# High and low value columns of a head side by side in one stationary operand, the cross part added on VectorE

## The reference

```
x: [8, 256, 256], ctx: [8, 256, 256]
h = layernorm(x)
h = layernorm(h + attention(h, h,   mask))       # 16 heads of 64
h = layernorm(h + attention(h, ctx, mask))
h = layernorm(h + gelu(h @ fc1_w + fc1_b) @ fc2_w + fc2_b)
x = x + h
y = layernorm(x)
x = x + geglu(y, shared) + geglu(y, expert chosen by argmax(y @ Wg))   # 8 experts

attention(x, c, mask):
    q, k, v = x @ wq, c @ wk, c @ wv
    out = softmax(mask(q @ k.T / 8)) @ v         # per head
    return out @ wo + bo
```

## Time and profile before

| | us |
|---|---|
| median of 3 runs | 1401.46 |
| the profiled execution | 1397.69 |
| its span, first to last instruction | 1395.9 |
| PE busy | 1353.5 |
| DVE busy | 965.5 |
| ACT busy | 815.4 |
| POOL busy | 532.1 |
| mean granted TensorE clock | 0.991 of full |

### The profile page before, as it was taken

The page is one execution under the profiler, slowest core; times in us unless marked ns, Lnnn a source line. Parts: engine busy times, 40 slices in busy tenths (PEclk is TensorE's granted clock), DMA queues, the critical chain, the costliest instruction groups (busy, mean ns, idle before and its releaser), DMA issues.

```text
span 1395.9 us, 32853 instructions
## 1 busy us (share of the span) xinstructions
PE 1353.5 (97%) x11598; PEld 1305.0 (93%) x11598; DVE 965.5 (69%) x2677; ACT 815.4 (58%) x2212; POOL 532.1 (38%) x913
## 2 busy tenths in 40 slices
PE   4999999999999999999999989999999999999999
PEld 3899999999998999999999989899999999999998
DVE  5777777777787777777777784434447777777754
ACT  3666766666666666766676665333226656565632
POOL 3644535444467444443443577655150000000040
PEclk9999999999999999999999999999999999999999
DMA  5060000000000004000000101010044666566521
GB/s 173 2 247 16 12 7 17 17 1 17 24 2 24 24 2 174 24 2 24 24 9 17 32 4 43 31 31 8 2 166 140 201 212 210 191 204 212 197 69 62
DMA packets 65185, 100.30 MB, mean 72 GB/s; under 512 B 4736, under 2 KB 53504, under 8 KB 65024
## 3 DMA queue, kind: packets, MB, share of 16 engines
q1 hardware_dynamic: 63488, 94.00, 20.2%
q0 software_dynamic: 1536, 4.20, 0.9%
HBM read 81.93 MB, written 16.25 MB: 70 GB/s over the span
## 4 chain that ended last, share of the span: by engine, by line
PE 88%; POOL 5%; DVE 3%; ACT 2%; issue 2%; DVEq 0%; ACTq 0%; POOLq 0%
PE ps_pj L47 10%; PE ps_pj L48 9%; PE ps_pj L49 9%; PE ps_t L797 9%; PE ps_s L787 7%; PE ps_pv L47 6%; PE ps_pv L49 6%; PE ps_pv L48 6%; PE ps_s L47 4%; PE ps_aux L47 4%; PE ps_aux L48 4%; PE ps_aux L49 4%; PE ps_s L49 4%; PE ps_s L48 4%; PE ps_t L830 1%
## 5 line engine op out<-in xcount | busy, mean ns | idle before, releaser
L555 POOL TENSOR_SCALAR probs<-probs,inv 128x256 f32<-128x256 f32 x512 | 241.9, 487 | 387.8 <-DVE inv L1227 387.5
L1028 ACT ACTIVATE probs<-scores,nb 128x256 f32<-128x256 f32 x512 | 255.1, 500 | 227.8 <-DVE nb L1217 213.2
L1217 DVE CUSTOM_DVE_ANT_0 scores<-ps_s,maskf 128x256 f32<-128x256 f32 x512 | 187.0, 421 | 64.8 <-PE ps_s L787 63.6
L1231 DVE TENSOR_TENSOR probs_t_lo<-ps_t,probs_t_hi 128x512 fp32r<-128x512 f32 x256 | 175.6, 686 | 14.1 <-ACT probs_t_hi L1035 2.6
L1089 ACT ACTIVATE gelu<-ps_pj 128x512 f32<-128x512 f32 x92 | 55.0, 598 | 189.0 <-PE ps_pj L49 189.0
L797 PE MATMUL ps_t<-ident,probs 128*128 128x128 f32 x1024 | 142.6, 282 | 12.2 <-POOL probs L555 12.2
L1277 DVE TENSOR_TENSOR ps_s<-ps_s,gelu 128x512 f32<-128x512 f32 x92 | 64.4, 700 | 126.2 <-PE ps_s L49 126.1
L1035 ACT ACTIVATE probs_t_hi<-ps_t 128x512 fp32r<-128x512 f32 x256 | 148.5, 580 | 3.3 <-PE ps_t L797 3.3
L47 PE MATMUL ps_pv<-probs_t_hi,vpad_lo 128*128 128x256 f32 x512 | 145.5, 284 | 0.0
L48 PE MATMUL ps_pv<-probs_t_lo,vpad_hi 128*128 128x256 f32 x512 | 145.2, 283 | 0.0
L49 PE MATMUL ps_pv<-probs_t_hi,vpad_hi 128*128 128x256 f32 x512 | 145.1, 283 | 0.0
(11 more groups left out here) (228 smaller groups left out, 4706.9 us busy)
## 6 DMA issues: line engine op xcount, KB each, us to landing
raw<-in_L_ffn_W SPq DMA_DIRECT2D x45, 1024.0 KB, 4.8
slot_rows<-hin SPq DMA_DIRECT2D x5, 768.0 KB, 7.2
xin<-slot_rows SPq DMA_DIRECT2D x15, 256.0 KB, 6.2
slot_out<-hin SPq DMA_DIRECT2D x15, 256.0 KB, 6.0
rows<-in_x SPq DMA_DIRECT2D x8, 256.0 KB, 2.7
after_self<-rows SPq DMA_DIRECT2D x8, 256.0 KB, 2.1
rows<-after_self SPq DMA_DIRECT2D x8, 256.0 KB, 2.6
cin<-in_ctx SPq DMA_DIRECT2D x8, 256.0 KB, 3.0
```

What stands on the lines that cost most here:

```text
L555: last = pool.tensor_scalar(PR[:, h, t, :], PR[:, h, t, :], inv[:, h, t:t + 1], 1.0, ALU.mult, ALU.mult)
L1028: last = act.activation(PR[:, h, t, :], SM[:, h, t, :], ACT.Exp, bias=nb[:, h, t:t + 1], scale=-1.0, accum_out=sums[:, h, t:t + 1])
L1217: last = dve.tensor_tensor_reduce(SM[:, h, t, :], ps_s[h][:, t * S:(t + 1) * S], maskf[:, i // PAIRS % 2, :], -SCALE, -LOWEST, ALU.add, AL ...
L1231: dve.tensor_tensor(flat(PT[1][:, i % 2, h, :, :]), ps_t[h][:, :], flat(PT[0][:, i % 2, h, :, :]).bitcast(F32), ALU.subtract).then_inc(t_l ...
```

## The change

`VP`, the padded values, becomes `VS`: for each head and block of keys one stationary operand of 128 columns, of which the first 64 are the high parts of the values and the last 64 their low parts. `attend` multiplies it by the low and then by the high part of the probabilities, and gives each head 256 columns of `ps_pv`. Rows 0 to 63 then hold the high values by the whole probabilities, rows 64 to 127 the low values by them, which is the cross part (with low by low, which was left out before).

ACT copies rows 64 to 127 of the bank into `cross` (`cross_of_pair`). DVE adds them to rows 0 to 63 in `joined`, one addition for each head (`join_pair`). `hi_of_pair` and `lo_of_pair` now read `joined` in SBUF, one pair later, and stand at other places of the loops. The values are split with one instruction of 128x512 on each engine in place of two of 128x256, and the clears at the start are gone.

```diff
             def attend(i):
                 g, p = i // 2, i % PAIRS
                 pe.wait_ge(pj_lo, EVENT[("v", g)] + 1)
-                wait(pe, o_lo, i)
+                wait(pe, joined_ready, i)
                 for h in range(2):
                     pe.wait_ge(t_lo, 2 * i + h + 1)
                     for j in range(ST):
-                        last = product(pe, ps_pv[:, 0:S], tuple(v[:, g % 2, j, 2 * (i % 2) + h, :] for v in VP),
-                                       tuple(x[:, i % 2, h, j, :] for x in PT), h == 0 and j == 0, h == 1 and j == ST - 1)
+                        v = VS[:, g % 2, j, 2 * (i % 2) + h, :, :].rearrange("p s d -> p (s d)")
+                        for x in (PT[1], PT[0]):
+                            last = pe.matmul(ps_pv[:, h * S:(h + 1) * S], v, x[:, i % 2, h, j, :], start=h == 0 and j == 0 and x is PT[1],
+                                             stop=j == ST - 1 and x is PT[0], skip_group_check=True)
                 last.then_inc(pv_done, 1)
...
-                    for odd in range(2):
-                        last = act.activation(vpad_half(VP[0], k, odd), v_half(bank, odd), ACT.Copy)
+                    last = act.activation(v_part(k, 0), v_rows(bank), ACT.Copy)
...
+            def cross_of_pair(i):
+                act.wait_ge(pv_done, i + 1)
+                act.activation(flat(cross[:, :, :]), ps_pv[DH:P, :], ACT.Copy).then_inc(cross_ready, 1)
+
             def hi_of_pair(i):
-                act.wait_ge(pv_done, i + 1)
+                act.wait_ge(joined_ready, i + 1)
                 wait(act, out_done, i - 3)
-                act.activation(OT[0][:, i % 4, :], ps_pv[:, 0:S], ACT.Copy).then_inc(o_hi, 1)
+                act.activation(OT[0][:, i % 4, :], joined[:, i % 2, :], ACT.Copy).then_inc(o_hi, 1)
...
                 hi_of_probs(i, 0)
+                if i >= 2:
+                    hi_of_pair(i - 2)
                 if i + 1 < NPAIR:
                     exps(i + 1, 1)
                 if i + 2 < NPAIR:
                     hi_of_bank(("qk", i + 2))
                 hi_of_probs(i, 1)
                 if i >= 1:
-                    hi_of_pair(i - 1)
+                    cross_of_pair(i - 1)
...
+            hi_of_pair(NPAIR - 2)
             gelu_dense(0)
+            cross_of_pair(NPAIR - 1)
             hi_of_pair(NPAIR - 1)
...
-                    for odd in range(2):
-                        last = dve.tensor_tensor(vpad_half(VP[1], k, odd), v_half(bank, odd),
-                                                 vpad_half(VP[0], k, odd).bitcast(F32), ALU.subtract)
+                    last = dve.tensor_tensor(v_part(k, 1), v_rows(bank), v_part(k, 0).bitcast(F32), ALU.subtract)
...
+            def join_pair(i):
+
+                dve.wait_ge(cross_ready, i + 1)
+                for h in range(2):
+                    last = dve.tensor_tensor(joined[h * DH:(h + 1) * DH, i % 2, :], ps_pv[0:DH, h * S:(h + 1) * S], cross[:, h, :], ALU.add)
+                last.then_inc(joined_ready, 1)
+
             def lo_of_pair(i):
                 dve.wait_ge(o_hi, i + 1)
-                dve.tensor_tensor(OT[1][:, i % 4, :], ps_pv[:, 0:S], OT[0][:, i % 4, :].bitcast(F32),
+                dve.tensor_tensor(OT[1][:, i % 4, :], joined[:, i % 2, :], OT[0][:, i % 4, :].bitcast(F32),
                                   ALU.subtract).then_inc(o_lo, 1)
...
-            for vp in VP:
-                dve.memset(vp[:, :, :, :, :].rearrange("p a b c d -> p (a b c d)").bitcast(F32), 0.0).then_inc(pad_ready, 1)
...
                 lo_of_probs(i, 0)
+                if i >= 2:
+                    lo_of_pair(i - 2)
                 if i + 1 < NPAIR:
                     invert_sums(i + 1, 1)
                 if i + 2 < NPAIR:
                     lo_of_bank(("qk", i + 2))
                 lo_of_probs(i, 1)
                 if i >= 1:
-                    lo_of_pair(i - 1)
+                    join_pair(i - 1)
...
+            lo_of_pair(NPAIR - 2)
+            late_hi_pieces(NPAIR + 1)
+            join_pair(NPAIR - 1)
             lo_of_pair(NPAIR - 1)
-            late_hi_pieces(NPAIR + 1)
```

More of the change, by code:

```diff
@@ L220, in fused @@
         PT = at("probs_t_hi", 104 * KB, [P, 2, 2, ST, S], F32R), at("probs_t_lo", 112 * KB, [P, 2, 2, ST, S], F32R)
-        VP = at("vpad_hi", 120 * KB, [P, 2, ST, HG, P], F32R), at("vpad_lo", 128 * KB, [P, 2, ST, HG, P], F32R)
+        VS = at("v_stack", 120 * KB, [P, 2, ST, HG, 2, DH], F32R)
+        cross, joined = at("cross", 128 * KB, [DH, 2, S]), at("joined", 130 * KB, [P, 2, S])
         QK = at("qk_hi", 136 * KB, [P, 2, 2, S], F32R), at("qk_lo", 144 * KB, [P, 2, 2, S], F32R)
@@ L257, in fused @@
         WB = [(W["k"], W["v"], tuple(t[:, :, :, :, :].rearrange("p a b c d -> p (a b c d)") for t in PT)),
-              (W["q"], W["o"], tuple(t[:, :, :, :, :].rearrange("p a b c d -> p (a b c d)") for t in VP))]
+              (W["q"], W["o"], (at("w3b_hi", 120 * KB, [P, WCOLS], F32R), at("w3b_lo", 128 * KB, [P, WCOLS], F32R)))]
         x2, normed = (stage[:, k * TT * D:(k + 1) * TT * D].rearrange("p (t d) -> p t d", d=D) for k in range(2))
@@ L295, in fused @@
         const_in, mask_in = sem("const_in"), sem("mask_in")
-        id_ready, pad_ready, half_ready, mask_ready = sem("id_ready"), sem("pad_ready"), sem("half_ready"), sem("mask_ready")
+        id_ready, half_ready, mask_ready = sem("id_ready"), sem("half_ready"), sem("mask_ready")
         first_in = {(k, q): sem(f"first_{k}{q}") for k in KINDS for q in range(GROUPS)}
@@ L308, in fused @@
         t_done, t_hi, t_lo = sem("t_done"), sem("t_hi"), sem("t_lo")
-        pv_done, o_hi, o_lo = sem("pv_done"), sem("o_hi"), sem("o_lo")
+        pv_done, cross_ready, joined_ready, o_hi, o_lo = (sem(n) for n in ("pv_done", "cross_ready", "joined_ready", "o_hi", "o_lo"))
         out_done, out_used = sem("out_done"), sem("out_used")
@@ L987, in _, with v_part, v_rows @@
                     down(step, range(FC))
[L989 to L994, removed]
+        def v_part(g, s):
+            return VS[:, g % 2, :, :, s, :].rearrange("p t h d -> p (t h) d")
+        def v_rows(bank):
+            return bank[:, :].rearrange("p (a d) -> p a d", d=DH)
         def flat(ap):
@@ L1011, in hi_of_bank @@
                 if kind == "v":
-                    if k == 0:
-                        act.wait_ge(pad_ready, 2)
                     wait(act, pv_done, 2 * (k - 1))
-                    for odd in range(2):
-                        last = act.activation(vpad_half(VP[0], k, odd), v_half(bank, odd), ACT.Copy)
+                    last = act.activation(v_part(k, 0), v_rows(bank), ACT.Copy)
                 elif kind == "qk":
```

## The result

The changed kernel takes 1435.54 us, the median of 4 runs (1434.51 to 1435.97), against 1401.32 us before (1401.15 to 1401.79, 4 runs). The ratio is 1.0243, with a 95% interval of 1.0225 to 1.026: 34 us slower. The span of the profiled execution went from 1395.9 to 1434.2 us, 38.3 us more; the profiled execution of before lay 3.6 us under its median, which is most of the difference between 34 and 38.

A forecast was written before the change was run, and what follows sets the result against it. PE was taken to bound attention at 6.23 us a plain pair, by only 0.33 us. Added ring work of 90.3 less 69.8 slack, +5 from the second ring and -2.5 at the start gave +23: 1424 us, range 1400 to 1442.

The forecast's parts named there:

- PE's step of 0.12 us, and 61 us taken from it: Attention, PE: a removed matmul gives back its 0.12 us step, not its 0.28 length; four per pair, 61 us in all.
- The two rings, 5.42 and 5.90 us: Plain pair: first ring, DVE and ACT, masked_max to masked_max, 5.42 us; second, leaving it for PE's scores, 5.90; PE 6.23.
- `hi_of_pair` in the ring, 0.32: ACT, between hi_of_probs(i, 0) and exps(i+1, 1): the 128x256 copy from SBUF adds 0.32 us to both rings.
- The moved `lo_of_pair` and the split of values cost nothing: DVE waits: lo_of_pair's 0.34 us fits into 0.8, and the single 128x512 split saves 0.06 in a similar gap; both nothing.
- `cross_of_pair` costs nothing: ACT, where hi_of_pair stood, outside the ring: about 0.58 us open, done 0.2 us before join_pair needs it; no cost.
- `join_pair`, 0.75 us for the two steps: DVE, first ring: two 64x256 additions, 0.41 us between them and 0.34 after; less 0.33 removed, 0.42 added.
- held additions: Rival, DVE: both additions and the following masked_max don't overlap, 0.41 to 0.46 us each; 1434 us, chance 0.16.
- The clears at the start, -2.5 us: Start: two clears of 1.76 us go from ahead of the first statistics; 2.5 us saved, bounds 0 and 3.9.
- ACT's copy is free: Rival, ACT: exps(i+1, 1) has hidden slack, so only DVE's 0.42 us counts; 1386 us, chance 0.09.
- PE stays the bound: Rival, attention: both rings are slack, so PE's 61 us and 2.5 at the start are gained; 1338 us, chance 0.06.
- the clock falls: Rival, PE: gaps in each pair cost its full clock in stretches, some 60 us; 1480 us, chance 0.04.
- no effect: Rival, whole kernel: the sum is off by 20 the right way, time within 0.2% of 1401 us; chance 0.05.

The follow-up runs named there:

- e1: Kernel before with two of the three matmuls in attend, high values by low probabilities left out, nothing else changed: 1367.81 us against 1401.62.
- e3: Changed kernel with both additions of join_pair writing rows 0 to 63, head 1's sum going to a spare buffer: 1420.51 us.
- e2: Changed kernel with hi_of_pair(i-2) moved ahead of exps(i+1, 0) in ACT's loop: 1398.05 us.
- e6: Changed kernel with hi_of_pair early and output_stats and input_stats on DVE moved behind masked_max: ratio 0.9844 to the kernel before.
- e8: Changed kernel with hi_of_pair early and lo_of_pair(i-2) on DVE moved behind masked_max: ratio 0.9987 to the kernel before.
- e5: Changed kernel with both additions of join_pair writing rows 64 to 127, head 0's sum going to a spare buffer: ratio 1.0263 to the kernel before.
- e7: Kernel before with output_stats and input_stats on DVE moved behind masked_max: ratio 0.9992.

## Why the prediction was right, and by how much it was off

The direction and the range held, and so did the mechanism in the main: PE was the bound by a little, and the instructions added to the ring of DVE and ACT were paid in full. 1424 was forecast with a range of 1400 to 1442, and 1435.5 was measured, at the edge of the forecast's own bounds of 1415 to 1435. Of +23 us, 11 were missing. Two signs came out otherwise than said: DVE's waiting for `scores` vanished and did not only shrink, and DVE went to 86 to 87% and not to 83%. The first comes from which of the two rings is the longer one (see `join_pair` below), the second from additions and a subtraction on DVE that take longer than was counted.

- *PE's step of 0.12 us, and 61 us taken from it:* right in that a matmul's length of 0.28 us is no price: with all four gone from each pair and nothing added, e1 gained 34 us and not the 145 us of 512 lengths. PE had the 61 us free and spent more than that, 86 us, waiting for DVE.
- *The two rings, 5.42 and 5.90 us:* right. e1 laid the second bare at 5.90, and e3 at 6.21, where 5.90 and the copy's 0.31 make 6.21. e2 laid the first bare: 5.42 and 0.54 for the additions (0.87 less the 0.33 of the old subtraction) make its 5.96.
- *`hi_of_pair` in the ring, 0.32:* measured 0.31, and e2 took exactly that out of every pair.
- *The moved `lo_of_pair` and the split of values cost nothing:* right. `lo_of_pair` lies open for 0.60 us, not 0.41, but the wait of 0.8 us had room for it.
- *`cross_of_pair` costs nothing:* right for `join_pair`, which never waited for `cross` in the pairs read, but not for ACT. The copy reads rows 64 to 127 of its PSUM bank. All 120 of them between 60 and 860 us start 0.02 us after the end of the instruction before, and so does the next instruction that reads PSUM. The same instructions overlap by 0.09 to 0.11 us where they stand elsewhere. In a pair with an extra event that next one is `hi_of_bank`, outside the ring. In the 37 pairs without one, from the 8th on, it is `hi_of_probs(i, 0)`, in the ring. ACT in such a pair, and in the plain pair shown above:

```profile
182.48 0.19 ACT L1028 ACTIVATION_READ_ACCUMULATOR probs<-scores,nb 128x1 f32 x1
182.69 0.60 ACT L1035 ACTIVATE probs_t_hi<-ps_t 128x512 fp32r<-128x512 f32 x1
...
383.22 0.19 ACT L1028 ACTIVATION_READ_ACCUMULATOR probs<-scores,nb 128x1 f32 x1
383.31 0.57 ACT L1035 ACTIVATE probs_t_hi<-ps_t 128x512 fp32r<-128x512 f32 x1
```

  From `exps(i+1, 0)` to `hi_of_probs(i, 0)` it is 1.12 us in these 37 pairs and 1.00 in the 82 others from the 8th pair on; in the kernel before it is 1.00 in all 119. The same pairs are the longer ones in e2 to e6 and e8.
- *`join_pair`, 0.75 us for the two steps:* this is the term that was mis-sized. It measured 0.87. I let only one of the two steps go without overlap, though no row told the two apart; both do. With 0.87 the first ring gets 0.31 + 0.87 - 0.33 = 0.85 in place of 0.74, becomes 6.27 and is the longer one. The sum by its own formula: 122 x 0.85 - 69.8 = +34, less 2.5 at the start, and the 5 us that the second ring was to add fall away.
- That was the rival *held additions*, given 0.16 and 1434 us: it had the better mechanism, and the range held since it was drawn around both. The Trainium skill ("VectorE: DVE Perf Modes", section on two Vector instructions with no wait between them) had the rule, and here the traces agree with it: steps of 0.33 to 0.34 without a change of quadrant (e3, e5), 0.42 to 0.45 with it (e5 and the changed kernel). I held one step of the two where that section's rule holds both.
- *The clears at the start, -2.5 us:* the first `masked_max` starts at 16.95 us, before at 19.91: -3.0. DVE's first statistics, beside the earlier trace rows, now wait for the input:

```profile
3.49 0.75 DVE L1261 BATCH_NORM_STATS2 part<-rows 128x6 f32<-128x256 f32 x2 [0.97 <-DMA rows<-in_x]
```

- The sum against the trace: from the 8th pair on the pairs are 37.3 us longer together, the first seven 2.0, the start 3.0 shorter, the last stages 1.9 longer, which makes the 38.3 of the two spans. For all pairs that is 39.3, and 122 x 0.85 - 69.8 gives 34 of it. Some 4.5 more are the 37 pairs in which `hi_of_probs` comes 0.12 us later: 6.40 in place of 6.27 us for a plain one, 7.46 in place of 7.32 with statistics. That the copy of rows 64 to 127 causes this is read from the starts alone, from which instructions are late and which are not; no run moves or changes that copy.

Of the rivals, *ACT's copy is free* fell by e2, *PE stays the bound* by e1 and PE's waits, *the clock falls* by the clock of 1.00 in attention, *no effect* by the 34 us.

## What to carry to other kernels

An engine at 100% can have another chain right behind it: before counting a saving, add up the ring of dependences through the other engines, link by link from the starts in the timeline, and subtract. Here it was 0.33 us of 6.23, and the change took 0.48 from PE and put 0.85 into the ring. When the bound moves, the order of the loops has to move too: the copy's place was worth 37 us and the place of the statistics 19, both without one instruction less.

## What the runs showed of the hardware that was not expected

- On DVE an instruction that writes from another half of the partitions than the one before it does not overlap with it. The step behind a 64x256 addition is 0.33 to 0.34 us within one half and 0.42 to 0.45 us to the other, and behind a 128x512 subtraction 0.71 and not 0.60. It also holds a full-height instruction that starts at row 0.
- On ACT a 64x512 copy that reads rows 64 to 127 of a PSUM bank started 0.02 us after the end of its forerunner in all 120 cases, and so did the next instruction that read PSUM from row 0 (82 times `hi_of_bank`, 38 times `hi_of_probs` with exponentials from SBUF in between). The traces show where, not why.
- A DVE subtraction of 128x256 with two SBUF inputs takes 0.42 us with no POOL instruction open beside it. Behind one that is open and ends late it ends 0.25 to 0.29 us after that one: 0.60 us in the median where POOL normalises the probabilities, 1.5 at the longest. The same subtraction with one input in PSUM took 0.41 to 0.43 us throughout in the kernel before, beside POOL's instructions too.
- Two chips differed by 23 us for one kernel (1401.6 and 1424.5). The last stages took 591 to 593 us in the four traces of one (e5 to e8) and 566 to 568 in the six of the other, and their clock was 0.95 in e7 against 0.99 before.
